# A decoder layer on one core: scores of two tiles on 32-row parts in mid-slot, expert weights asked for inside the experts' block

## Chip, cores and metric

One core of one Trainium2 chip runs the whole layer. The metric is the device time of one execution in microseconds (us). Engines are TensorE (PE), VectorE (DVE), ScalarE (ACT), GpSimd (POOL) and SyncE (SP, which here only issues DMAs).

## The reference

Input `x` is [64, 64, 256] (64 sequences of 64 tokens) and `ctx` is [64, 64, 64]. Three residual steps follow each other, all fp32:

```python
x = x + attn(layernorm(x))           # causal, 16 query heads, 4 key/value groups, head size 16
x = x + xattn(layernorm(x), ctx, ctx)  # no mask; keys and values are ctx; then @ Wc.T + bc
x = x + ffn(layernorm(x))            # 64 experts, top 6 of the best 3 of 8 groups, 96 slots each, and a shared MLP
# attn, xattn: softmax(q @ k.T / 4) @ v, for each head and each of the 64 sequences
# ffn: an expert computes (silu(x @ Wg.T) * (x @ Wu.T)) @ Wd.T on its slots; the shared MLP the same with 352 columns
```

## The kernel before

The 4096 tokens are 32 tiles of 128 tokens; a tile holds two sequences, and four tiles are a group. The program is a row of blocks; between two blocks all engines meet at a barrier: (1) inputs and constants, (2) attention (`attention_phase`), (3) a block in which SyncE issues the loads of the shared weights (`sgu`, `sd`) and of the first 8 experts' weights, (4) a block in which GpSimd writes seven small constants, (5) shared MLP and experts (`moe_phase`), (6) the final sums. An SBUF region that attention used is given to the weights only after block 2.

Block 2 does self attention for tiles 0 to 31 and cross attention for 32 to 63 in one software pipeline. Each engine runs `for m in range(FIRST, LAST)`, and the order of the calls in this loop body is the order of its queue; nothing but semaphores ties the engines. I call one turn `m` a slot. For each tile there are: scores (TensorE, line 396 the mask as a bf16 product, line 401 queries by keys, into `Sc`), their maximum and shift (VectorE, lines 724 and 728, into `E`), the exponential in place (ScalarE, 639), eight 128x128 transposes of it (TensorE, 413), copies to SBUF (ScalarE, 600), the product with the values (TensorE, 429, into the single bank `O`), reciprocal and output (VectorE, 735 and 744). Self attention adds the output to `X` on GpSimd (909); cross attention transposes it (439), multiplies it by `Wc` (447) and adds it to `X` on VectorE (753), and then routes the token: a third layer norm, logits (466), their transpose (474), choice of groups and experts on VectorE and GpSimd, and a transpose of the weights (482).

Queries lie in `qT` as two chunks of 128 rows, 8 heads of 16 rows each. Keys are copied by DMA from `kT` into `kbd`, where each head's 16 rows meet only the 64 columns of their own head, zeros elsewhere; this is 16 DMAs a group (line 275), all issued by SyncE, each with 16 partitions. TensorE's array is used in four parts of 64 by 64: `r` is the half of the rows, `b` the sequence. One product takes 64 rows (4 heads) and gives 256 columns. `Sc` has two buffers of two banks, used by tiles in turn. A product in fp32 goes through the array in two passes, so counts in the profile are twice those of the program.

Every other result of TensorE goes through a ring of 3 banks in the fixed order of `ring_uses` (unchanged); a bank is filled again when ScalarE or VectorE has saved the use three before.

Per slot TensorE does, in this order: scores of tile m+1, transpose of the output of m-2, transposes of tile m's exponentials, the `Wc` product of m-2, one or more of the group's projections and routing steps (by `m % 4`), and the value product of m-1. VectorE: maximum and shift of m+1, layer norm statistics, residual of m-2, reciprocal and output of m-1, routing steps. ScalarE: copies of tile m, layer norms and keys, exponential of m+1, queries.

## Time and profile before

| | us |
|---|---|
| median of 3 runs | 809.72 (807.61 to 810.27) |
| the profiled execution | 804.97 |
| its span | 803.2 |
| PE busy | 669.4 (83%) |
| PE weight loads busy | 483.4 (60%) |
| DVE busy | 479.0 (60%) |
| POOL busy | 351.2 (44%) |
| ACT busy | 337.6 (42%) |

Busy times are sums over the whole span. The probability transposes of tile 0 start at 41.51, those of tile 32 at 201.43; attention's last instruction on an engine ends at 434.96, and the experts' first matmul starts at 445.27. The granted clock is TensorE's, as a share of 2.4 GHz: 1.00 or 0.50 in any moment, 0.91 on average. "Idle before" in a row is how long the engine did nothing before it, with what ended the wait. A matmul's shown time contains its way through the array, so rows that follow closely overlap; what one costs is the distance from start to start.

### The profile page before, as it was taken

Reading aid. Unit: us, or ns where it says so; the run is one execution under the profiler, and the core shown is the slowest. Engines: PE = TensorE matmul, PEld = TensorE weight load, DVE = VectorE, ACT = ScalarE, POOL = GpSimd, SP = SyncE. Lnnn points to the kernel's source line nnn. Section 1 sums busy time; section 2 is a strip of 40 time slices with the busy share of each in tenths; the row PEclk is TensorE's granted clock in tenths of the full one; section 3 lists DMA queues with packets and bytes.
Section 4 is the critical chain, followed back from the end, with each engine's and each line's share of the span. In section 5 each row is a group of like instructions: output and inputs, shape, how many; then the busy total and the mean of one; then the engine's idle time right before and its main releaser. Section 6 shows DMA issues by size and latency. Waiting matters only on the chain. (4 is left out here: it accounts for less than half of the span.)

```text
span 803.2 us, 16833 instructions
## 1 busy us (share of the span) xinstructions
PE 669.4 (83%) x6353; PEld 483.4 (60%) x6353; DVE 479.0 (60%) x1087; ACT 337.6 (42%) x636; POOL 351.2 (44%) x356
## 2 busy tenths in 40 slices
PE   1699999997899897889761899979999999987093
PEld 0366666665676665657530355557788789976072
DVE  3267776677788687777753899742333334433058
ACT  2477777766687576565521232211222222221000
POOL 5021122225444234243120383383777777757354
PEclk9899999999999899998965799989999999999555
DMA  7234444554533232231113500013999999994299
GB/s 229 26 58 82 82 81 82 101 96 89 111 71 66 48 71 57 35 60 35 33 40 93 184 0 1 0 49 106 233 237 252 242 239 252 275 254 62 29 320 314
DMA packets 112063, 94.26 MB, mean 117 GB/s; under 512 B 59760, under 2 KB 95856, under 8 KB 111984
## 3 DMA queue, kind: packets, MB, share of 16 engines
q1 hardware_dynamic: 96368, 74.57, 36.7%
q0 software_dynamic: 10240, 14.16, 9.5%
q10 hardware_dynamic: 5376, 4.46, 1.8%
q8 instruction: 51, 0.84, 0.5%
q14 instruction: 28, 0.23, 0.1%
HBM read 60.26 MB, written 24.50 MB: 106 GB/s over the span
## 5 line engine op out<-in xcount | busy, mean ns | idle before, releaser
L1230 POOL DMA_INDIRECT sum_d<-nz,targets x64 | 91.8, 1434 | 40.5 <-DMA sum_d<-nz,targets 11.9
L724 DVE TENSOR_REDUCE mx<-Sc 128x16 f32<-128x1024 f32 x64 | 77.8, 1216 | 33.4 <-PE Sc L401 33.2
L1057 PE MATMUL bank<-xnT,sgu_sb 128*128 128x512 f32 (+1 forms) x192 | 87.7, 606 | 11.7 <-PEq L1593 11.7
L1112 PE MATMUL bank<-xT,wgu_sb 128*88 128x96 f32 x1024 | 95.8, 247 | 0.3 <-ACT xT L1181 0.3
L1112 PEld LDWEIGHTS bank<-xT,wgu_sb 128*88 128x88 f32 x1024 | 90.0, 158 | 0.6 <-issue 0.5
L600 ACT COPY ET<-ring 128x512 f32<-128x512 f32 x128 | 69.3, 589 | 42.5 <-PE ring L413 40.4
L1281 DVE TENSOR_TENSOR hid<-sil,bank 88x192 f32<-88x192 f32 x64 | 22.4, 350 | 104.2 <-ACT sil L1187 104.2
L413 PE MATMUL ring<-ident,E 128*128 128x128 f32 x512 | 72.6, 286 | 14.3 <-ACT E L639 13.4
L429 PEld LDWEIGHTS O<-vbd,ET 128*64 128x64 f32 x2048 | 69.2, 142 | 25.1 <-issue 17.2
L728 DVE TENSOR_TENSOR E<-Sc,mx 128x1024 f32<-128x1024 f32 x64 | 78.4, 1225 | 6.9 <-DVE mx L724 0.5
L639 ACT ACTIVATE E<-E 128x1024 f32<-128x1024 f32 x64 | 67.5, 1055 | 29.7 <-DVE E L728 29.5
L401 PE MATMUL Sc<-kbd,qT 64*64 64x256 f32 x1024 | 75.2, 399 | 4.5 <-DMA kbd<-kT 4.5
L413 PEld LDWEIGHTS ring<-ident,E 128*128 128x128 f32 x512 | 58.9, 146 | 30.8 <-ACT E L639 21.3
L429 PE MATMUL O<-vbd,ET 128*64 128x34 f32 x2048 | 76.4, 229 | 0.0
L1223 POOL DMA_INDIRECT xg<-rows_d,tokens x64 | 61.9, 967 | 27.9 <-issue 15.1
L1057 PEld LDWEIGHTS bank<-xnT,sgu_sb 128*128 128x128 f32 (+1 forms) x192 | 35.6, 186 | 54.0 <-issue 52.7
L909 POOL TENSOR_TENSOR X<-X,att 128x256 f32<-128x256 f32 x32 | 23.2, 726 | 101.7 <-DVE att L744 101.7
L1123 PE MATMUL bank<-wd_sb,hid 88*96 88x256 f32 x256 | 66.8, 384 | 0.0
L1063 PE MATMUL bank<-sd_sb,hT 128*128 128x256 f32 (+1 forms) x192 | 47.1, 398 | 6.6 <-POOL hT L1211 5.8
L735 DVE RECIPROCAL rc<-O 128x16 f32<-128x16 f32 x64 | 16.3, 255 | 56.9 <-PE O L429 56.7
L1181 ACT COPY xT<-bank 128x192 f32<-128x192 f32 x64 | 20.2, 318 | 71.1 <-PE bank L1100 71.1
L1405 PE MATMUL bank<-lastsb,wt 64*128 64x256 f32 x64 | 26.1, 636 | 26.6 <-DMA lastsb<-lasts_d 26.6
(152 smaller groups left out, 1139.0 us busy)
## 6 DMA issues: line engine op xcount, KB each, us to landing
wgu_sb<-in_wgu_dram SPq DMA_DIRECT2D x64, 352.0 KB
wd_sb<-in_wd_dram SPq DMA_DIRECT2D x64, 176.0 KB
sum_d<-zeros SPq DMA_DIRECT2D x16, 524.0 KB, 6.3
y<-sum_d SPq DMA_DIRECT2D x16, 512.0 KB, 8.8
kbd<-kT SPq DMA_DIRECT2D x248, 32.0 KB, 2.1
X<-in_x_dram SPq DMA_DIRECT2D x8, 512.0 KB, 6.5
rows_d<-xhT SPq DMA_DIRECT2D x8, 512.0 KB, 3.0
out_dram<-X ACTq DMA_DIRECT2D x8, 512.0 KB, 4.8
```

The source lines that it names most:

```text
L401: last = nc.tensor.matmul(Sc[m % 2][64 * b:64 * (b + 1), r, 256 * c:256 * (c + 1)], qT[rows, g % 2, c, at:at + 64], kbd[g % 2][rows, c, 2 ...
L413: last = nc.tensor.transpose(out[:, 128 * j:128 * (j + 1)], E_[:, m % 2, at:at + 128], ident[:])
L429: last = nc.tensor.matmul(O[64 * b:64 * (b + 1), 2 * VW * pair:2 * VW * (pair + 1)], ET[:, m % 2, j, 64 * b:64 * (b + 1)], vbd[:, g % 2, 2 ...
L600: nc.scalar.copy(ET[:, m % 2, 4 * v:4 * v + 4].rearrange("p j q -> p (j q)"), bank(name)[:]).then_inc(s_act, 1)
L639: nc.scalar.activation(E_[:, m % 2, :], E_[:, m % 2, :], ACT.Exp).then_inc(s_exp, 1)
L724: nc.vector.reduce_max(mx[:, m % 2, :], sc, AX.X).then_inc(s_mx, 1)
L728: nc.vector.tensor_tensor(E_[:, m % 2, :].rearrange("p (h k) -> p h k", k=S), sc, mx[:, m % 2, :].unsqueeze(2).to_broadcast([128, H, S]), ...
L1057: last = nc.tensor.matmul(out[0:m, :], sgu[:, e, k * MS + m0:k * MS + m0 + m], xnT[:, e, TOK * g:TOK * (g + 1)], start=e == 0, stop=e == 1)
L1112: last = nc.tensor.matmul(GP[e % 2][0:MH, CAP * u:CAP * (u + 1)], wgu[:, j, 4 * MH * c + MH * u:4 * MH * c + MH * (u + 1)], xT[:, e % 2, c ...
L1123: last = nc.tensor.matmul(DP[e % 2][0:CAP, 0:E], hid[:, e % 2, u, :], wd[:, j, E * u:E * (u + 1)], start=u == 0, stop=u == 1)
L1223: pool.indirect_dma_start(xg[:, j, :], None, w["rows"], bass.IndirectOffsetOnAxis(ap=tokens[:, e:e + 1], axis=0)).then_inc(s_g[j], 16)
L1230: pool.indirect_dma_start(w["sums"][e % 2], bass.IndirectOffsetOnAxis(ap=targets[:, e:e + 1], axis=0), outs[:, e % EB, :], None, compute_o ...
```

## The change

1. Scores are computed for two tiles in one call, `scores(p)` for tiles 2p and 2p+1. The array is used in eight parts: four strips of 32 rows (`r`, 2 heads each) by two halves of columns (`b`). One product takes 32 rows and gives 128 columns. Strip `r` writes bank `r` of `Sc`, which is now one buffer of four banks; tile n of the pair takes columns 256n to 256n+255 of each. The heads' order in `Sc` follows, and `pair_of` with it. The mask is 512 columns wide and is multiplied once for both tiles.
2. In TensorE's slot the value product of m-1 is now first; the scores stand behind the transposes of tile m, in even slots only, for tiles m+2 and m+3, and wait until both tiles before them are shifted.
3. Blocks 3 and 4 are gone. Their loads are the first DMAs, and their constants the first GpSimd instructions, of block 5; TensorE waits there for the three shared loads, VectorE for the constants where it uses them.

```diff
@@ -103,8 +103,8 @@
 def pair_of(j):
 
-    r, c, m = j // 4, j // 2 % 2, j % 2
-    return 4 * c + 2 * r + m
+    r, c = j // 2, j % 2
+    return 4 * c + r
 
@@ -381,27 +381,32 @@
                 last.then_inc(s_fill, 1)
 
-            def scores(m):
-                g, t = m // GT, m % GT
+            def scores(p):
+                g, t = 2 * p // GT, 2 * p % GT
                 cross = is_cross(g)
                 if t == 0:
                     pe.wait_ge(s_kbd, KDMA * (g + 1))
                     pe.wait_ge(*saved(("XT1" if cross else "Q1", g)))
-                if m >= 2:
-                    pe.wait_ge(s_sub, m - 1)
-                for c in range(2):
-                    if not cross:
-                        for r, b in ((0, 0), (1, 0), (0, 1), (1, 1)):
-                            rows = slice(64 * r, 64 * (r + 1))
-                            nc.tensor.matmul(Sc[m % 2][64 * b:64 * (b + 1), r, 256 * c:256 * (c + 1)],
-                                             ident_bf[rows, rows], mask[rows, :], start=True, stop=False)
-                    for r, b in ((0, 0), (1, 0), (0, 1), (1, 1)):
-                        rows = slice(64 * r, 64 * (r + 1))
-                        at = 128 * t + 64 * b
-                        last = nc.tensor.matmul(Sc[m % 2][64 * b:64 * (b + 1), r, 256 * c:256 * (c + 1)],
-                                                qT[rows, g % 2, c, at:at + 64],
-                                                kbd[g % 2][rows, c, 2 * t + b].rearrange("p h k -> p (h k)"),
-                                                start=cross, stop=True)
+                if p >= 1:
+                    pe.wait_ge(s_sub, 2 * p)
+                if not cross:
+                    for r in range(0, 4, 2):
+                        for k, b in ((0, 0), (1, 0), (0, 1), (1, 1)):
+                            rows = slice(64 * k, 64 * (k + 1))
+                            nc.tensor.matmul(Sc[64 * b:64 * (b + 1), r + k, :], ident_bf[rows, rows], mask[rows, :],
+                                             start=True, stop=False)
+                for n in range(2):
+                    for c in range(2):
+                        for b in range(2):
+                            at = 128 * (t + n) + 64 * b
+                            for r in range(4):
+                                rows = slice(32 * r, 32 * (r + 1))
+                                last = nc.tensor.matmul(
+                                    Sc[64 * b:64 * (b + 1), r, 256 * n + 128 * c:256 * n + 128 * (c + 1)],
+                                    qT[rows, g % 2, c, at:at + 64],
+                                    kbd[g % 2][rows, c, 2 * (t + n) + b, 2 * (r % 2):2 * (r % 2) + 2].rearrange(
+                                        "p h k -> p (h k)"), start=cross, stop=cross or (n == 1 and c == 1),
+                                    tile_position=(32 * r, 64 * b))
                 last.then_inc(s_sc, 1)
@@ -484,12 +489,14 @@
             pe.wait_ge(s_in, n_in)
             for m in range(FIRST, LAST):
-                if 0 <= m + 1 < 2 * NT:
-                    scores(m + 1)
+                if 0 <= m - 1 < 2 * NT:
+                    pv(m - 1)
                 if crossed(m - 2):
                     out_t(m - 2)
                 if 0 <= m < 2 * NT:
                     probs_t(m)
+                if m % 2 == 0 and 0 <= m + 2 < 2 * NT:
+                    scores(m // 2 + 1)
                 if crossed(m - 2):
@@ -520,8 +527,6 @@
                     if routed((m - 8) // 4):
                         logits((m - 8) // 4)
-                if 0 <= m - 1 < 2 * NT:
-                    pv(m - 1)
 
@@ -719,14 +724,15 @@
 
             def shift(m):
-                dve.wait_ge(s_sc, m + 1)
-                sc = Sc[m % 2][:].rearrange("p r (h k) -> p (r h) k", k=S)
-                nc.vector.reduce_max(mx[:, m % 2, :], sc, AX.X).then_inc(s_mx, 1)
+                dve.wait_ge(s_sc, m // 2 + 1)
+                sc = Sc[:, :, 256 * (m % 2):256 * (m % 2 + 1)].rearrange("p r (h k) -> p r h k", k=S)
+                nc.vector.reduce_max(mx[:, m % 2, :].rearrange("p (r h) -> p r h", r=4), sc, AX.X).then_inc(s_mx, 1)
                 if m >= 2:
                     dve.wait_ge(s_fill, ring.filled(("TP1", m - 2)))
                 dve.wait_ge(s_mx, m + 1)
-                nc.vector.tensor_tensor(E_[:, m % 2, :].rearrange("p (h k) -> p h k", k=S), sc,
-                                        mx[:, m % 2, :].unsqueeze(2).to_broadcast([128, H, S]),
+                nc.vector.tensor_tensor(E_[:, m % 2, :].rearrange("p (r h k) -> p r h k", r=4, k=S), sc,
+                                        mx[:, m % 2, :].rearrange("p (r h) -> p r h", r=4).unsqueeze(3).to_broadcast(
+                                            [128, 4, 4, S]),
                                         ALU.subtract).then_inc(s_sub, 1)
@@ -989,6 +995,9 @@
         return k if e % 2 == 0 and k < len(LATE) else None
 
+    s_in = sem("shared_weights")
+    s_one = sem("columns")
+    s_slot = sem("slots")
     s_up = sem("up")
@@ -1036,6 +1045,12 @@
                 sp.dma_start(w["lasts"][e:e + 1, :], outs[CAP - 1:CAP, e % EB, :]).then_inc(s_l[e % EB], 16)
 
+            sp.dma_start(sgu[:], w["sgu"].rearrange("(c p) n -> p c n", p=128)).then_inc(s_in, 16)
+            sp.dma_start(sd[:, 0:2, :], w["sd"][0:256].rearrange("(c p) n -> p c n", p=128)).then_inc(s_in, 16)
+            sp.dma_start(sd[0:MS - 256, 2, :], w["sd"][256:MS]).then_inc(s_in, 16)
+            for j in range(EB):
+                sp.dma_start(wgu[:, j, :], w["wgu"][j]).then_inc(s_w[j], 16)
+                sp.dma_start(wd[:, j, :], w["wd"][j]).then_inc(s_w[j], 16)
             for e in range(NE):
@@ -1124,7 +1139,7 @@
                 last.then_inc(s_d, 1)
 
-            pe.wait_ge(w["s_moe_in"], w["n_moe_in"])
+            pe.wait_ge(s_in, 48)
             early_up(0)
@@ -1231,6 +1246,15 @@
                                         outs[:, e % EB, :], None, compute_op=ALU.add).then_inc(s_s[e % 2], 16)
 
+            nc.gpsimd.iota(slot[:], pattern=[[1, CAP]], base=0, channel_multiplier=0,
+                           allow_small_or_imprecise_dtypes=True).then_inc(s_slot, 1)
+            nc.gpsimd.memset(own[:], 1.0).then_inc(s_one, 1)
+            nc.gpsimd.memset(lastone[:], 0.0).then_inc(s_one, 1)
+            nc.gpsimd.memset(lastrow[:], 0.0).then_inc(s_one, 1)
+            pool.wait_ge(s_one, 3)
+            for m, fill in ((own, 0.0), (lastone, 1.0), (lastrow, float(NT * 128 + CAP - 1))):
+                nc.gpsimd.affine_select(out=m[:], in_=m[:], compare_op=ALU.not_equal, fill=fill, base=-(CAP - 1),
+                                        pattern=[[0, 1]], channel_multiplier=1).then_inc(s_one, 1)
             hidden(0)
@@ -1325,6 +1349,7 @@
             nc.vector.tensor_scalar(mark[NE:128, :], top[NE:128, :], 0.0, None, ALU.is_equal).then_inc(s_tok, 1)
             dve.wait_ge(s_tok, 4)
+            dve.wait_ge(s_slot, 1)
             nc.vector.tensor_tensor(mark[NE:128, :], mark[NE:128, :], slot[NE:128, :], ALU.mult).then_inc(s_tok, 1)
@@ -1337,6 +1362,7 @@
             dve.wait_ge(s_tt, 1)
             nc.vector.tensor_copy(tokens[:], P[0][0:CAP, 0:NE]).then_inc(s_list, 1)
+            dve.wait_ge(s_one, 6)
             nc.vector.tensor_scalar(targets[:], P[0][0:CAP, 0:NE], own[:], lastrow[:], ALU.mult,
@@ -1472,7 +1498,7 @@
         mem["zeros"] = zeros = sb("zeros", [128, E + NE])
         mem["ident_bf"] = sb("ident_bf", [128, 128], BF16)
-        mem["mask"] = sb("mask", [128, HQ * S], BF16)
+        mem["mask"] = sb("mask", [128, HH * S], BF16)
         mem["halfmask"] = sb("halfmask", [128, 2])
@@ -1501,7 +1527,7 @@
         w["ctx2"] = sb("ctx2", [128, 2, GB, G * D])
 
-        mem["Sc"] = [pb(f"Sc{k}", [128, 2, 512]) for k in range(2)]
+        mem["Sc"] = pb("Sc", [128, 4, 512])
         mem["O"] = pb("O", [128, 512])
@@ -1528,7 +1553,7 @@
                     pool.wait_ge(s_const, h + 1)
                     nc.gpsimd.affine_select(out=m, in_=m, compare_op=ALU.is_ge, fill=MASKED,
-                                            base=0, pattern=[[0, HQ], [-1, S]],
+                                            base=0, pattern=[[0, HH], [-1, S]],
                                             channel_multiplier=1).then_inc(s_const, 1)
@@ -1568,19 +1593,6 @@
-        s_iota = ctx.enter_context(nc.semaphore("router_constants"))
-        w["s_moe_in"] = ctx.enter_context(nc.semaphore("shared_weights"))
-        w["n_moe_in"] = 48
-        with nc.Block() as block:
-            @block.sync
-            def _(sp):
-                sp.dma_start(w["sgu_sb"][:], sgu.rearrange("(c p) n -> p c n", p=128)).then_inc(w["s_moe_in"], 16)
-                sp.dma_start(w["sd_sb"][:, 0:2, :], sd[0:256].rearrange("(c p) n -> p c n", p=128)).then_inc(w["s_moe_in"], 16)
-                sp.dma_start(w["sd_sb"][0:MS - 256, 2, :], sd[256:MS]).then_inc(w["s_moe_in"], 16)
-                for j in range(EB):
-                    sp.dma_start(w["wgu_sb"][:, j, :], wgu[j]).then_inc(w["s_w"][j], 16)
-                    sp.dma_start(w["wd_sb"][:, j, :], wd[j]).then_inc(w["s_w"][j], 16)
...
@@ -1590,19 +1602,6 @@
-        with nc.Block() as block:
-            @block.gpsimd
-            def _(pool):
-                nc.gpsimd.iota(mem["slot"][:], pattern=[[1, CAP]], base=0, channel_multiplier=0,
...
```

On TensorE, the self half, from the keys projection of a group (`wkv_sb`) to the second query projection's neighbours; `ring<-ident,E` are the probability transposes, `O<-vbd,ET` the value products. Before:

```order
L356 MATMUL ring<-xhT,wkv_sb 128x512 x2
L429 MATMUL O<-vbd,ET 64x34 x16
L396 MATMUL Sc<-mask,ident_bf 64x256 x4
L401 MATMUL Sc<-kbd,qT 64x256 x4
L396 MATMUL Sc<-mask,ident_bf 64x256 x4
L401 MATMUL Sc<-kbd,qT 64x256 x4
L413 MATMUL ring<-ident,E 128x128 x8
L356 MATMUL ring<-xhT,wq_sb 128x512 x2
L429 MATMUL O<-vbd,ET 64x34 x16
```

and now:

```order
L356 MATMUL ring<-xhT,wkv_sb 128x512 x2
L434 MATMUL O<-vbd,ET 64x34 x16
L418 MATMUL ring<-ident,E 128x128 x8
L396 MATMUL Sc<-mask,ident_bf 64x512 x8
L404 MATMUL Sc<-kbd,qT 64x128 x32
L356 MATMUL ring<-xhT,wq_sb 128x512 x2
L434 MATMUL O<-vbd,ET 64x34 x16
L418 MATMUL ring<-ident,E 128x128 x8
```

The scores of one tile that stood between value products and transposes are gone from there; a pair's stand behind the transposes.

On TensorE, the cross half, one slot with `m % 4` = 0 of a routed group; `ring<-ident,att` is the transpose of the output, `wc_sb` the output projection, `gate` the logits. Before:

```order
L429 MATMUL O<-vbd,ET 64x34 x16
L401 MATMUL Sc<-kbd,qT 64x256 x8
L439 MATMUL ring<-ident,att 128x128 x2
L413 MATMUL ring<-ident,E 128x128 x8
L447 MATMUL ring<-wc_sb,oT 128x256 x2
L348 MATMUL ring<-ident,xh 128x128 x4
L466 MATMUL ring<-xnT,gate 64x512 x2
L429 MATMUL O<-vbd,ET 64x34 x16
```

and now:

```order
L434 MATMUL O<-vbd,ET 64x34 x16
L444 MATMUL ring<-ident,att 128x128 x2
L418 MATMUL ring<-ident,E 128x128 x8
L404 MATMUL Sc<-kbd,qT 64x128 x32
L452 MATMUL ring<-wc_sb,oT 128x256 x2
L348 MATMUL ring<-ident,xh 128x128 x4
L471 MATMUL ring<-xnT,gate 64x512 x2
L434 MATMUL O<-vbd,ET 64x34 x16
```

The scores moved from ahead of both transposes to between the transposes and the output projection, and the value products from the slot's end to its head.

## Rows read from the trace of the kernel before

**Rows 1.** TensorE in order of time, self half, one group: start us, us, what, [idle before]

```profile
117.54 1.10 PE L413 MATMUL ring<-ident,E 128*128 128x128 f32 x8
118.47 1.88 PE L356 MATMUL ring<-xhT,wkv_sb 128*128 128x512 f32 x4
120.28 1.13 PE L429 MATMUL O<-vbd,ET 128*64 128x34 f32 x32
121.34 0.30 PE L396 MATMUL Sc<-mask,ident_bf 64*64 64x256 bf16 x4
...
123.34 1.09 PE L413 MATMUL ring<-ident,E 128*128 128x128 f32 x8 [0.72 <-ACT E L639]
...
127.14 0.30 PE L396 MATMUL Sc<-mask,ident_bf 64*64 64x256 bf16 x4
...
128.34 1.09 PE L413 MATMUL ring<-ident,E 128*128 128x128 f32 x8
...
133.91 1.09 PE L413 MATMUL ring<-ident,E 128*128 128x128 f32 x8
...
138.27 1.10 PE L413 MATMUL ring<-ident,E 128*128 128x128 f32 x8
```

**Rows 2.** The key DMAs: SyncE's issues of one group; issues by size and us to landing

```profile
121.10 11.02 SPq L275 DMA_DIRECT2D kbd<-kT  x16
...
kbd<-kT SPq DMA_DIRECT2D x248, 32.0 KB, 2.1
```

**Rows 3.** TensorE where it waits for the key DMAs

```profile
195.95 1.09 PE L401 MATMUL Sc<-kbd,qT 64*64 64x256 f32 x16 [2.80 <-DMA kbd<-kT]
...
213.72 1.19 PE L401 MATMUL Sc<-kbd,qT 64*64 64x256 f32 x16 [1.68 <-DMA kbd<-kT]
...
215.31 1.91 PE L413 MATMUL ring<-ident,E 128*128 128x128 f32 x8
```

**Rows 4.** Engines per stretch: us, busy (instructions) PE, PEld, DVE, ACT, POOL, clock, DMA

```profile
197.91:218.37 20.46, 17.53 (x248) 13.82 (x247) 16.60 (x30) 14.13 (x26) 10.79 (x11) 0.92 0.58 115
218.37:237.40 19.03, 18.11 (x260) 14.28 (x259) 16.78 (x36) 14.74 (x28) 7.38 (x11) 1.00 0.40 78
260.14:288.97 28.83, 24.86 (x279) 18.63 (x278) 21.70 (x70) 17.66 (x35) 10.57 (x14) 0.88 0.28 55
```

**Rows 5.** TensorE in order of time, cross half, no routing

```profile
219.74 1.09 PE L401 MATMUL Sc<-kbd,qT 64*64 64x256 f32 x16
220.79 0.41 PE L439 MATMUL ring<-ident,att 128*128 128x128 f32 x2
...
221.91 1.03 PE L447 MATMUL ring<-wc_sb,oT 128*128 128x256 f32 x4
```

**Rows 6.** VectorE in order of time, cross half, no routing

```profile
224.85 0.42 DVE L744 TENSOR_TENSOR att<-O,rc 128x256 f32<-128x256 f32 x1
...
227.03 1.22 DVE L728 TENSOR_TENSOR E<-Sc,mx 128x1024 f32<-128x1024 f32 x1
...
233.13 0.41 DVE L753 TENSOR_TENSOR X<-ring,X 128x256 f32<-128x256 f32 x1
...
233.81 0.42 DVE L744 TENSOR_TENSOR att<-O,rc 128x256 f32<-128x256 f32 x1
```

**Rows 7.** All engines in order of time, cross half, fully routed group

```profile
275.89 0.41 DVE L753 TENSOR_TENSOR X<-ring,X 128x256 f32<-128x256 f32 x1
...
276.35 1.11 PE L482 MATMUL ring<-ident,wa 128*128 128x128 f32 x4 [2.46 <-DVE X L753]
```

**Rows 8.** All engines between attention and experts; the shared weights' landing

```profile
436.19 0.46 SPq L1579 DMA_DIRECT2D sd_sb<-in_sd_dram  x1
...
444.08 0.22 POOL L1596 IOTA slot<- 128x96 f32 x1 [11.77 <-DVEq L1593]
...
445.27 1.19 PE L1057 MATMUL bank<-xnT,sgu_sb 128*128 128x512 f32 x1 [11.72 <-PEq L1593]
...
sd_sb<-in_sd_dram SPq DMA_DIRECT2D x1, 96.0 KB, 4.6
```

18 lines of the change are left out of this document (4 added, 14 removed).

## Prediction

> **What bounds the kernel now.** I read the time in four stretches, and the change touches two of them: attention (0 to 435 us) and the gap between attention and the experts (435 to 445 us). I call turn `m` of the attention loop a slot; A, B, C, D are the slots with `m % 4` = 0, 1, 2, 3, and four slots serve one group of four tiles.
>
> In the self half TensorE is the bound. In [rows 1] the probability transposes, once per slot, start 5.80, 5.00, 5.57 and 4.36 us apart, 20.73 for a group, and the only idle time is 0.72 us in front of slot A's. It waits there for ScalarE, which must first copy this group's keys and values out of the bank: keys projection at 118.47, transposes at 123.34, held by the exponential of line 639. Keys then go through 16 DMAs that SyncE issues one after the other in 11.02 us, each landing 2.1 us after its issue [rows 2]: at 118.47 plus 15.1 to 15.8.
>
> In the cross half the bound moves. Two groups wait for those DMAs; after one such wait of 1.68 us the granted clock was at its lower level, 1.2 GHz, and eight transposes took 1.91 us for 1.09 [rows 3]. A group without routing takes 19.03 us, one with all of it 28.83 us at a mean granted clock of 0.88 [rows 4]. In the latter VectorE is 21.70 us busy, against 16.78, and TensorE sits 2.46 us waiting for VectorE's residual addition to free a bank [rows 7]. So the cross half is a loop between TensorE and VectorE, and its order matters more than TensorE's work.
>
> **Scores of two tiles at once.** A tile's scores cost 1.20 us in the self half (127.14 to 128.34) [rows 1], 1.05 us in the cross half (219.74 to 220.79) [rows 5]. Each of 4 array parts then streams 4 times 256 fp32 columns. Now each of 8 parts streams 8 times 128 columns for a pair of tiles: as many columns a part, twice the tiles. So a pair should cost what one tile did, 1.05 us; in the self half the mask passes keep their columns (0.15 a tile, so 0.30) and one more change of part size is passed, for which I take 0.1: 1.45 us. That saves 1.05 and 0.95 us a pair. The bound above: the value products issue 32 passes in 1.06 us (120.28 to 121.34) [rows 1], 33 ns each, and a pair now has 64: 2.1 us, no saving. I take the lower end, since those passes have 34 columns and load new weights each, and share the array by 2 where this has 8 parts.
> The Trainium skill, "TensorE: Matmul & The Clock Gate", section "Wait — 56ns, not 53.3ns?", has a rule against such small pieces: where the sequencer decodes in microcode, each matmul takes it 62 ns, whatever its columns; by that, 64 would cost 4.0 us a pair and the whole come to some 60 us more. The 33 ns of the value products disagree with it here, so it changes no term, and its chance is under 0.01, inside rival (c).
>
> **The new order, self half.** A slot's own work is unchanged but for the scores: A 5.00 - 1.20 + 1.45 = 5.25, B 5.57 - 1.20 = 4.37, C 4.36 - 1.20 + 1.45 = 4.61, D 5.80 - 0.72 - 1.20 = 3.88: 18.1 us for 20.73. But two things do not get shorter. (1) Slot A's transposes wait for ScalarE until 123.34 - 118.47 = 4.87 us after the keys projection began. Before, value products and one tile's scores (2.26) filled this; now only value products stand there (the scores moved behind the transposes), so TensorE idles 4.87 - 1.81 - 1.06 = 2.0 us where it idled 0.72. Period: 20.1. (2) The first scores of a group now come in slot C, not at the start of D. From the keys projection to there it is 4.87 + 0.93 + 1.45 + 1.81 + 4.37 + 1.99 = 15.4 us, and the DMAs land after 15.1 to 15.8: a wait of 0 to 0.4. So a group takes 20.1 to 20.5, and six of them save 2.4 us of the 15 that the work alone would give. The start costs the 1.45 us of the first pair, which now stands as a whole ahead of the value transposes and the second keys: +1.4. And an idle stretch of 2.0 us can cost the clock: it fell after 1.68 in [rows 3], and not after every such wait. That one lasted some 3.3 us (a mean clock of 0.92 over the 20.46 us around it [rows 4]) and cost up to half of that: 1.7. I count two among the six groups, +3.4. Self half together: +2.4.
>
> **Cross half.** Here VectorE's maximum and shift of slot m's next tile must be done before the pair's scores in A and C (one buffer instead of two), the output projection `wc` stands behind these scores, VectorE's residual behind `wc`, then reciprocal and output, and TensorE's value products, now first in the slot, behind the output. It is one chain through both engines. From output to output in A or C: end of output to end of shift 2.98 (225.27 to 228.25) [rows 6], to the scores 0.1, scores 1.05, `wc` 1.03 [rows 5], residual to end of output 1.10 (233.13 to 234.23) [rows 6] and 0.05 between: 6.3. In B or D: 0.1, value products 1.06, transposes 1.12 (220.79 to 221.91), `wc` 1.03, 1.15: 4.5. Two of each are 21.6 us for a group without routing, where [rows 4] has 19.03: +2.6. The groups before it wait for DMAs anyway, and value products now lie between the scores and the next keys: +1.1 and, with the residual's chain, +1.8; the partly routed one +0.5. A fully routed group adds VectorE's 21.70 - 16.78 = 4.9 us in the same chain: 26.5; 1.0 for falls of the clock, which the old ones have too: 27.5 for 28.83, 28.0 and 28.3 (the two routed groups that follow it), so -2.7 for three. In the last two groups and the drain no next scores hold the chain, and the last value products come ahead of `wc` (1.03) and of a logits projection (4 passes of 0.43) instead of behind them: 3 us, and 2 for scores and shifts that no longer alternate; -5, between -2 and -7. Cross half: +1.1 + 1.8 + 2.6 + 0.5 - 2.7 - 5 = -1.7.
>
> **Between attention and experts.** The last attention instruction but a DMA ends at 435; the last piece of the shared weights is asked for at 436.19, but TensorE starts at 445.27, since SyncE first issues 16 more weights, then the block ends, then GpSimd writes its constants in another [rows 8]. Now TensorE waits for the shared weights alone: issue at 436.19 and 4.6 us to landing: 440.8. Gain 4.4. VectorE starts its 12 rounds of maxima 10 us earlier, but they ended ahead of TensorE before, so this gives nothing more. GpSimd's seven small constants lie beside that wait. All behind it is bound by TensorE's own queue and shifts as a whole. The longer mask costs GpSimd up to 1 us at the very start, while VectorE clears the key buffer until 5.4: nothing; without that cover, 1 us.
>
> **Sum.** +2.4 - 1.7 - 4.4 = -3.7 on the profiled 804.97 (span 803.2 and 1.8 around it), which lies 4.75 below the median of the three runs, 809.72. On the median: **806.0**. A difference of 0.3%, 2.4 us, is about what a measurement of this kernel can tell from none.
>
> **Rivals.**
> (a) *The clock falls in every self group.* The 2.0 us idle ahead of slot A is new in each. Eight falls of 1.7 us instead of two: +10.2, so 816. For it: the row after 1.68 us of waiting. Against: the wait of 2.80 us ahead of 195.95 left the clock alone [rows 3]. It decides against the change from about four falls on.
> (b) *The cross loop is looser than I chain it.* If VectorE runs a slot ahead and the scores find their buffer free, groups with routing are bound by VectorE's work or TensorE's, some 22 to 24 us, and those without stay at 19: 27.5 becomes 23 for each of three, -13.5, and the 2.6 of the group without routing may stay as well: 790 to 793. For it: VectorE waits for value products in all groups now, and no more then. Against: the shift stands behind the output in VectorE's own queue [rows 6].
> (c) *The eight parts do not run side by side*, so the change does not do what it says: a pair costs 2.1 and all 32 pairs lie on a chain: +1.0 each, 838. Against: four parts do so now, eight transfers of weights are small.
> (d) *The gap does not close*: the weights land later, as 17 transfers share the queues: +4.4, 810. Against: these same transfers were in flight before.
>
> **Chances.** Forecast 0.48 (its own range 798 to 811: DMA wait 0 to 0.4 a group, falls of the clock 0 to 4, drain -2 to -7), (a) 0.18, (b) 0.20, (c) 0.07, (d) 0.04, the rest 0.03. Faster by over 0.3% (below 807.3): 0.29 of the forecast's, all of (b), a little of (a): 0.51. Within: 0.21. Slower: 0.28. Range: 791 to 817, which leaves out (c) and the far ends.
>
> **What would show it.** Right: a pair of scores in about 1.05 us (cross) and 1.45 (self); 2.0 us idle ahead of every slot A's transposes in the self half, with ScalarE's exponential named; group periods of 20.1 to 20.5, then 21.6, then 26 to 28; TensorE waiting for VectorE's shift ahead of the scores and for its output ahead of the value products; the experts' first matmul 5.6 us after attention ends. Wrong: self groups of 18 us (ScalarE's chain shorter than read) or over 21 (clock); routed groups near 22 or over 29; a pair's scores at 2 us.

## The result, and the profile after

| | before | changed |
|---|---|---|
| median of 4 runs, us | 808.71 (807.61 to 810.27) | 817.89 (815.08 to 818.63) |
| ratio to before | | 1.0106, 95% interval 1.0074 to 1.0138 |
| profiled execution, us (span) | 804.97 (803.2) | 818.63 (816.9) |

The changed kernel is 1.1% slower. It was forecast at 806.0 us in a range of 791 to 817. The two profiled spans differ by 13.7 us, more than the medians (9.2): the profiled execution of before was faster than all four of the table, and that of the changed kernel was the slowest of its four. The page of the changed kernel:

```profile
span 816.9 us, 18604 instructions
...
PE 652.5 (80%) x7249; PEld 482.8 (59%) x7249; DVE 475.0 (58%) x1087; ACT 339.0 (41%) x636; POOL 352.1 (43%) x356
...
L434 PE MATMUL O<-vbd,ET 128*64 128x34 f32 x2048 | 75.2, 227 | 21.4 <-DVE att L750 18.6
...
L418 PE MATMUL ring<-ident,E 128*128 128x128 f32 x512 | 71.2, 284 | 16.8 <-ACT E L644 16.4
...
L404 PE MATMUL Sc<-kbd,qT 32*64 32x128 f32 x2048 | 44.0, 308 | 24.0 <-DVE E L733 16.7
```

And two lines of the page before:

```profile
L401 PE MATMUL Sc<-kbd,qT 64*64 64x256 f32 x1024 | 75.2, 399 | 4.5 <-DMA kbd<-kT 4.5
...
L429 PE MATMUL O<-vbd,ET 128*64 128x34 f32 x2048 | 76.4, 229 | 0.0
```

TensorE's own work fell from 669.4 to 652.5 us, the scores alone from 75.2 us (1024 passes) to 44.0 (2048 passes), and the kernel still got slower: the time went into waits, named at the end of the rows. TensorE was idle for 4.5 us ahead of scores and not at all ahead of value products; now it is 24.0 and 21.4 us, most of it spent on VectorE. The same group of the self half as in [rows 1], TensorE in order of time (start us, us, what, [idle before]):

```profile
131.44 1.10 PE L418 MATMUL ring<-ident,E 128*128 128x128 f32 x8 [1.93 <-ACT E L644]
132.47 0.63 PE L396 MATMUL Sc<-mask,ident_bf 64*64 64x512 bf16 x8
133.02 1.21 PE L404 MATMUL Sc<-kbd,qT 32*64 32x128 f32 x64
134.16 1.98 PE L356 MATMUL ring<-xhT,wq_sb 128*128 128x512 f32 x4
...
152.56 0.66 PE L418 MATMUL ring<-ident,E 128*128 128x128 f32 x4 [1.93 <-ACT E L644]
```

A pair's scores take 0.55 us for the mask and 1.14 for 64 passes (132.47, 133.02, 134.16). With two such pairs, and with 1.93 us of idle time ahead of slot A for 0.72, a group takes 21.12 us for 20.73. TensorE where the cross half waits, against [rows 3] and [rows 5]:

```profile
207.03 2.01 PE L404 MATMUL Sc<-kbd,qT 32*64 32x128 f32 x64 [4.05 <-DMA kbd<-kT]
208.97 1.93 PE L434 MATMUL O<-vbd,ET 128*64 128x34 f32 x32
210.83 1.97 PE L418 MATMUL ring<-ident,E 128*128 128x128 f32 x8
...
227.86 1.21 PE L404 MATMUL Sc<-kbd,qT 32*64 32x128 f32 x64 [1.94 <-DMA kbd<-kT]
...
238.87 1.21 PE L404 MATMUL Sc<-kbd,qT 32*64 32x128 f32 x64 [0.53 <-DVE E L733]
...
242.44 1.13 PE L434 MATMUL O<-vbd,ET 128*64 128x34 f32 x32 [0.87 <-DVE att L750]
...
250.70 1.21 PE L404 MATMUL Sc<-kbd,qT 32*64 32x128 f32 x64 [1.36 <-DMA kbd<-kT]
```

The first cross group's keys now cost a wait of 4.05 us for 2.80, and the value products behind it take 1.93 us for 1.13. The second group's keys cost 1.94 us for 1.68. In the group without routing TensorE waits for VectorE's shift (0.53), for its output (0.87) and once more for keys (1.36). Three stretches follow, as in [rows 4]: 10 us from the last microsecond of the first wait on, the group without routing, and the first fully routed one:

```profile
206.00:216.00 10.00, 8.13 (x138) 7.19 (x138) 6.58 (x12) 3.74 (x7) 4.28 (x4) 0.50 0.75 148
237.30:260.70 23.40, 17.95 (x333) 15.14 (x331) 17.41 (x38) 15.95 (x30) 8.89 (x11) 1.00 0.34 67
284.66:313.21 28.55, 22.15 (x345) 17.71 (x344) 21.75 (x71) 17.98 (x33) 10.83 (x14) 0.94 0.29 57
```

The clock was at 1.2 GHz (0.50) in all of the first; no such stretch followed the 2.80 us of [rows 3]. The group without routing takes 23.40 us (19.98 before, from the transposes of slot 36 to those of slot 40), the routed one 28.55 (29.10 before, 264.82 to 293.92). The end of attention and the start of the experts, for [rows 8]:

```profile
450.43 0.69 DVE L827 SCALAR_TENSOR_TENSOR keys<-desc,ring 64x512 f32<-64x512 f32 x1 [2.80 <-ACT wt L640]
451.41 0.39 SPq L1048 DMA_DIRECT2D sgu_sb<-in_sgu_dram  x1
...
452.36 0.46 SPq L1050 DMA_DIRECT2D sd_sb<-in_sd_dram  x1
...
457.90 2.08 PE L1072 MATMUL bank<-xnT,sgu_sb 128*128 128x512 f32 x2 [8.18 <-DMA sd_sb<-in_sd_dram]
```

All engines are through the barrier 0.3 us after attention's last instruction (451.13), and TensorE starts 6.8 us behind it, for 10.3: the blocks' merging gave 3.5 us. The account by stretches; a stretch is given by the slots whose transposes begin and end it:

| stretch | changed minus before, us | forecast |
|---|---|---|
| start to slot 0 | +2.3 | +1.4 |
| slots 0 to 24 (six self groups) | +6.6 | +1.0 |
| 24 to 32 | +5.75 | +1.1 |
| 32 to 36 | +1.6 | +1.8 |
| 36 to 40 (no routing) | +3.4 | +2.6 |
| 40 to 44 | +0.2 | +0.5 |
| 44 to 56 (three routed groups) | -2.5 | -2.7 |
| 56 to attention's end | -1.2 | -5 |
| gap | -3.5 | -4.4 |
| experts to the end | +1.0 | 0 |

### The profile page after: what moved, and what is told of

Same layout as the page of the kernel before. It is cut to its first block and busy times, and to the rows that moved or that the text cites. A ratio compares the mean times of both kernels' runs of the same rounds, so it can differ in the third digit from the quotient of the medians.

```text
span 816.9 us, 18604 instructions
## 1 busy us (share of the span) xinstructions
PE 652.5 (80%) x7249; PEld 482.8 (59%) x7249; DVE 475.0 (58%) x1087; ACT 339.0 (41%) x636; POOL 352.1 (43%) x356
## 5 line engine op out<-in xcount | busy, mean ns | idle before, releaser
L434 PE MATMUL O<-vbd,ET 128*64 128x34 f32 x2048 | 75.2, 227 | 21.4 <-DVE att L750 18.6
L418 PEld LDWEIGHTS ring<-ident,E 128*128 128x128 f32 x512 | 58.3, 144 | 20.2 <-ACT E L644 18.1
L404 PE MATMUL Sc<-kbd,qT 32*64 32x128 f32 x2048 | 44.0, 308 | 24.0 <-DVE E L733 16.7
L404 PEld LDWEIGHTS Sc<-kbd,qT 32*64 32x64 f32 x2048 | 35.5, 148 | 35.0 <-issue 16.0
L1202 ACT ACTIVATE sil<-bank 88x192 f32<-88x192 f32 x64 | 20.9, 326 | 77.5 <-PE bank L1127 66.3
L1078 PEld LDWEIGHTS bank<-sd_sb,hT 128*128 128x128 f32 (+1 forms) x192 | 38.1, 200 | 15.3 <-issue 9.6
```

The source lines that it names most:

```text
L404: last = nc.tensor.matmul(Sc[64 * b:64 * (b + 1), r, 256 * n + 128 * c:256 * n + 128 * (c + 1)], qT[rows, g % 2, c, at:at + 64], kbd[g % 2 ...
L418: last = nc.tensor.transpose(out[:, 128 * j:128 * (j + 1)], E_[:, m % 2, at:at + 128], ident[:])
L434: last = nc.tensor.matmul(O[64 * b:64 * (b + 1), 2 * VW * pair:2 * VW * (pair + 1)], ET[:, m % 2, j, 64 * b:64 * (b + 1)], vbd[:, g % 2, 2 ...
L1078: last = nc.tensor.matmul(out, hT[0:m, c, 128 * t:128 * (t + 1)], sd[0:m, c, :], start=c == 0, stop=c == 2)
```

## The experiments

Each was timed against the kernel before on the same chip; ratios are to that kernel. One ratio is uncertain by 0.3 to 0.4%, and so a difference between two of them by some 3 to 4 us. The changed kernel stands at 1.0106.

### Merged blocks alone

Edit: parts 1 and 2 of the change left out, part 3 kept.

> The kernel before with the merged blocks alone. Theory: the gap between attention and the experts closes as it did in the changed kernel, 10.3 us before, 6.8 us there, and nothing else moves: 3.5 us faster than before. Rival: the earlier start is partly given back behind it, because in the changed kernel the stage from the experts' first matmul to the end took 359.0 us for 357.9: 2.4 us faster, and second rival, all of it is given back: no difference.

Measured: ratio 0.9961, interval 0.9928 to 0.9993, some 3 us less; attention's end to the experts' first matmul 437.02 to 443.13, 6.1 us. The blocks' merging is a gain near the 3.5 us expected; the first rival's 2.4 cannot be told from it. The new scores alone therefore cost 1.0106 / 0.9961, 11.7 us, uncertain by some 4. That is what has to be explained.

### The new order with the old parts

```diff
+            def scores(p):
                 if p >= 1:
                     pe.wait_ge(s_sub, 2 * p)
...
                 for n in range(2):
-                    for c in range(2):
...
+                    tile_scores(2 * p + n)
```

`tile_scores` is the old function for one tile, with 64-row parts and two banks, without its wait for the shift; the layout of `Sc`, `pair_of` and the mask are the old ones.

> The changed kernel (merged blocks, pairs of scores in mid-slot, value product first) with the old parts of 64 rows and the old layout of the scores. Theory 'order': the place of the scores costs the time and the parts of 32 rows are a gain of their own, 0.96 us a pair in the cross half (2.10 for 1.14) and 0.5 in the self half (2.4 for 1.9): 16 x 0.96 + 16 x 0.5 = 23 us slower than the changed kernel, some 841. Theory 'parts': the small parts cost what the trace does not show and the order is harmless: no slower than the changed kernel, 818 or less.

Measured: 1.0398 (1.0355 to 1.0440), 23.5 us slower than the changed kernel. TensorE in the self half (a pair in C, then slot A) and the cross half (a pair):

```profile
155.01 0.30 PE L394 MATMUL Sc<-mask,ident_bf 64*64 64x256 bf16 x4
...
157.30 0.66 PE L348 MATMUL ring<-ident,xh 128*128 128x128 f32 x4
...
165.66 1.97 PE L417 MATMUL ring<-ident,E 128*128 128x128 f32 x8 [1.93 <-ACT E L643]
167.56 0.43 PE L394 MATMUL Sc<-mask,ident_bf 64*64 64x256 bf16 x4
...
255.58 1.96 PE L399 MATMUL Sc<-kbd,qT 64*64 64x256 f32 x32 [0.53 <-DVE E L732]
257.46 1.13 PE L451 MATMUL ring<-wc_sb,oT 128*128 128x256 f32 x4
```

A pair on 64-row parts takes 2.29 us in the self half (155.01 to 157.30, 1.69 on 32-row parts) and 1.88 in the cross half (1.14). The small parts are a gain of 0.6 us a pair in the self half and 0.75 in the cross half. For the cross half I had expected 0.96. If all pairs lay on the path, 16 x 0.75 + 16 x 0.6 = 22 us would be the whole, but part of the 23.5 is the clock: the transposes behind 1.93 us of idle time take 1.90 us (165.66 to 167.56) in slots 0, 4, ... 24, in all seven, where the changed kernel has three such slots. Four more falls of 1.5 us are 6 us. So the expected sum was hit by another mix, which is luck. What holds is that the small parts are a gain and the order is the loss: with the same 64-row parts, the new order is 35 us slower than the merged blocks alone.

### Pairs on small parts at the head of the odd slots

```diff
-                if 0 <= m - 1 < 2 * NT:
-                    pv(m - 1)
+                if m % 2 == 1 and 0 <= m + 1 < 2 * NT:
+                    scores((m + 1) // 2)
                 if crossed(m - 2):
                     out_t(m - 2)
                 if 0 <= m < 2 * NT:
                     probs_t(m)
-                if m % 2 == 0 and 0 <= m + 2 < 2 * NT:
-                    scores(m // 2 + 1)
...
+                if 0 <= m - 1 < 2 * NT:
+                    pv(m - 1)
```

> The changed kernel with pairs of scores on 32-row parts at the head of the odd slots (tiles m+1 and m+2) and the value product back at the slot's end. Theory 'order': TensorE no longer waits in mid-slot for VectorE's shift, the first scores of a group stand again where they stood, a slot later, so that the key DMAs have landed in the self half and cost 2.8 and 1.7 us again instead of 4.05, 1.94 and 1.36: at least 12 us faster than the changed kernel, 800 to 806. Theory 'parts': the order is harmless, the same as the changed kernel within 3 us, 815 to 821. The idle time of about 2 us ahead of slot A's transposes is expected to stay by both, since no scores stand at the head of slot A.

Measured: 1.0134 (1.0094 to 1.0174), 2 us above the changed kernel and not separable from it. The expectation "order" fell. The first wait for keys was gone, but the second had become 3.48 us. A self group took 20.86 us for the old 20.73: what the group saved on the scores stood as idle time ahead of slot A (1.93 for 0.72). And the routed groups became longer than in either kernel (29.1 before, 28.55 changed). The first of them, and its waits:

```profile
271.11:302.68 31.57, 24.93 (x344) 20.32 (x343) 22.18 (x72) 17.95 (x33) 10.81 (x14) 0.79 0.28 55
```

```profile
282.63 1.11 PE L487 MATMUL ring<-ident,wa 128*128 128x128 f32 x4 [2.34 <-DVE X L759]
...
286.58 0.66 PE L444 MATMUL ring<-ident,att 128*128 128x128 f32 x2 [0.98 <-DVE att L750]
```

With less work of its own, TensorE only comes earlier to VectorE's residual addition (`X`) and output (`att`), idles 2.34 and 0.98 us there, and the clock of the group is 0.79. What the small parts save is worth nothing where VectorE or ScalarE sets the period. That the idle time also brings the lower clock is a reading of this trace; no run took it out here.

### Half of the cross half's key DMAs

```diff
-for c in range(1 if g == 0 else 2):
+for c in range(1 if g == 0 or g >= NG else 2):
```

The waits' counts follow. It leaves out the keys of heads 8 to 15 in cross attention. The second of the two runs has the same edit on the kernel with merged blocks and the old scores.

> The changed kernel, in which the cross half's keys are copied for the first 8 heads alone (8 DMAs a group instead of 16; the other heads' scores use what lies in the buffer). Theory 'key DMAs': the waits of 4.05, 1.94 and 1.36 us ahead of a group's first scores vanish, and the lower clock behind the first of them (a mean of 0.65 over the 15 us around it) with them: 8 to 10 us faster than the changed kernel. Rival 'chain': VectorE's shift, one buffer for two tiles, takes the place of each wait: 2 us faster at most.

> The kernel before with merged blocks, in which the cross half's keys are copied for the first 8 heads alone (8 DMAs a group; the other heads' scores use what lies in the buffer). In the changed kernel this was worth 10 us by the medians. Theory: the old order waits less for the key DMAs, 2.81 and 1.74 us in two groups and one fall of the clock of 1.7: at most 6 us faster than the same kernel with all keys, so that at least 4 of the changed kernel's loss are the earlier place of a group's first scores. Rival: it gains as much here, 10 us, and the place of the scores has nothing to do with it.

Measured: in the changed kernel 0.9981 (0.9954 to 1.0008), 10.1 us less; with the old scores and merged blocks 0.9865 (0.9830 to 0.9900) for 0.9961, 7.8 us less. Slots 24 to 44 took 110.97 us in the changed kernel and 99.39 with half its key DMAs, 100.15 with the old scores and 94.51 with half. So the key DMAs bound both orders: 11.6 us of these slots go in the new, 5.6 in the old. Of the 11.6, 1.5 is the fall of the clock in slot 24, ahead of any wait for these keys, and in the new order one wait of 0.89 us for keys remains. Of the 10.8 us between the two kernels 4.9 stay with half of the DMAs, which I put down to the new order's chain. The second result lies between its two cases, at most 6 us and 10, and by its uncertainty decides for neither.

### The idle time ahead of slot A filled

```diff
-                pe.wait_ge(s_exp, m + 1)
                 for v in range(2):
                     out = empty_bank((f"TP{v}", m))
+                    if v == 0:
+                        if m % 4 == 0 and m <= NT:
+                            for j in range(14):
+                                nc.tensor.transpose(out[:, 128 * (j % 4):128 * (j % 4 + 1)], ident[:], ident[:])
+                        pe.wait_ge(s_exp, m + 1)
```

> The changed kernel with 14 transposes of the identity, into the ring bank that the next real transposes overwrite, where TensorE idles 1.93 us ahead of slot A's transposes (tiles 0, 4, ... 32): some 1.6 us of filling that delays nothing. Theory 'clock': the lower clock in slot A (7.18 us instead of 5.69 in three of the seven groups of the changed kernel, in all seven of the one with parts of 64 rows) comes from this idle time: every slot A of the self half takes 5.69 us, 3 to 4.5 us faster than the changed kernel. Rival: the falls have another cause: they stay, and the time is the same or up to 1 us longer.

Measured: 1.0059 (1.0031 to 1.0086), 3.8 us less than the changed kernel, uncertain by 3.4. TensorE at slot 12, and slots 0 to 24 (busy times, clock, DMA), first with the filling:

```profile
106.14 1.75 PE L418 MATMUL ring<-ident 128*128 128x128 f32 x14
108.15 1.09 PE L422 MATMUL ring<-ident,E 128*128 128x128 f32 x8 [0.26 <-ACT E L648]
...
113.83 1.09 PE L422 MATMUL ring<-ident,E 128*128 128x128 f32 x8
```

```profile
44.03:171.58 127.55, 125.12 (x2077) 88.12 (x2077) 82.82 (x138) 92.27 (x144) 25.83 (x44) 1.00 0.40 77
```

And in the changed kernel:

```profile
43.80:173.69 129.89, 118.13 (x1992) 80.76 (x1993) 83.10 (x138) 92.25 (x144) 25.79 (x44) 0.97 0.42 75
```

With 1.75 us of useless transposes in the gap, slot A takes 5.7 us in all seven groups (108.15 to 113.83) and the mean clock is 1.00 for 0.97. In the changed kernel three slots A (0, 12, 24) took 7.18 us, 1.5 more, and three other kernels with the same self half have three such slots each. So the clock falls do come from this idle time: there is more work on the same path, and it takes less time.

### The value product first, scores tile by tile

```diff
             for m in range(FIRST, LAST):
+                if 0 <= m - 1 < 2 * NT:
+                    pv(m - 1)
                 if 0 <= m + 1 < 2 * NT:
                     scores(m + 1)
...
-                if 0 <= m - 1 < 2 * NT:
-                    pv(m - 1)
```

On the kernel with merged blocks.

> The kernel before with merged blocks and one move: the value product first in the slot, ahead of the next tile's scores, which stay per tile on 64-row parts. Theory 'value product': the shorter routed groups of the changed kernel (28.5, 27.0, 26.7 us against 29.1, 27.8, 27.9 before) and its shorter end come from this move: the same lengths here, 3 us faster than the merged blocks alone; the self half keeps its 20.7 us a group. Rival 'pairs': they come from scores computed once in two slots: groups of 28 to 29 us here, no faster than the merged blocks alone or slower.

Measured: 1.0492 (1.0455 to 1.0529), 43 us slower than the merged blocks alone. The rival allowed for slower, but with routed groups of 28 to 29 us; these took 26.05, 25.14 and 26.05 us, less than in any kernel so far. Both follow from one chain. TensorE and VectorE over one self slot:

```profile
149.22 1.13 PE L429 MATMUL O<-vbd,ET 128*64 128x34 f32 x32 [1.32 <-DVE att L744]
150.28 0.30 PE L396 MATMUL Sc<-mask,ident_bf 64*64 64x256 bf16 x4
...
151.48 1.09 PE L413 MATMUL ring<-ident,E 128*128 128x128 f32 x8
...
155.55 0.27 PE L429 MATMUL O<-vbd,ET 128*64 128x34 f32 x3 [0.69 <-DVE att L744]
```

```profile
148.65 0.42 DVE L744 TENSOR_TENSOR att<-O,rc 128x256 f32<-128x256 f32 x1
151.63 1.22 DVE L724 TENSOR_REDUCE mx<-Sc 128x16 f32<-128x1024 f32 x1 [2.56 <-PE Sc L401]
152.96 1.22 DVE L728 TENSOR_TENSOR E<-Sc,mx 128x1024 f32<-128x1024 f32 x1
...
154.65 0.23 DVE L735 RECIPROCAL rc<-O 128x16 f32<-128x16 f32 x1
154.98 0.42 DVE L744 TENSOR_TENSOR att<-O,rc 128x256 f32<-128x256 f32 x1
```

The scores end at 151.5. VectorE's maximum and shift follow, 1.22 us each; behind them in its queue stand statistics (not shown), the reciprocal and the output, which ends at 155.4. Only then comes TensorE's next value product (it waits 0.69 for `att`), and behind that the next scores. The chain goes round once in every slot, 6.33 us, where a self slot has 4.4 to 5.6 of work. The changed kernel has the same chain, but with scores in only one of two slots; that this is what the pairs are good for is argued and not tested. A routed slot of the merged blocks alone takes 7 us on average. There the chain costs nothing, and TensorE's waits for `X` in three routed groups shrink from 10.2 us in total to 1.8.

### The new order only from slot 42 or 44 on

Two versions on the kernel with merged blocks. The first switches to the changed kernel's pairs for tiles 44 and up, the second only calls `pv(m - 1)` first from slot 44 on:

```diff
             for m in range(FIRST, LAST):
+                if 44 <= m and m - 1 < 2 * NT:
+                    pv(m - 1)
...
-                if 0 <= m - 1 < 2 * NT:
+                if 0 <= m - 1 < 43:
                     pv(m - 1)
```

> The old scores (64-row parts, tile by tile at the head of the slot, value product at its end) for tiles 0 to 43, pairs on 32-row parts in mid-slot with the value product first from tile 44 on, and the merged blocks. Theory: the new order and parts are worth what the two traces show for the routed groups and the end (slot 44 to the last keys 166.5 us in the changed kernel, 170.1 before), and the loss lies all ahead of them: 3.7 for this and 3.5 for the blocks, 7 us faster than before. Rival: the gain there hangs on the state in which the loop enters, or is lost in the scatter of the clock: no faster than the merged blocks alone, 3.5 us faster than before.

> The kernel before with merged blocks, and the value product first in the slot from slot 44 on (before that at the slot's end). Theory: where the value product stands first for the whole loop, TensorE and VectorE form one chain a slot (maximum, shift, output, value product, scores: 6.3 us), which costs much in the self half and nothing where a slot takes 6.3 us anyway; there it shortened a routed group from 29.2, 27.8 and 27.8 us to 26.1, 25.1 and 26.1, and slot 60 to the last keys from 58 to 60 us to 52.5. So from slot 44 on 7.5 + 2.3 + 6 = 16 us less, 1 to 2 of them lost at the change of order: 14 us faster than the merged blocks alone, 18 faster than before. Rival: the short groups hang on the long ones ahead of them, that is on work already done when the loop arrives: at most 4 us faster than the merged blocks alone.

Measured: 0.9953 (0.9926 to 0.9979) for the pairs, no more than the merged blocks alone (0.9961), so the rival held. In its trace slot 42, where the order changes, took 10.47 us for 5.96. And 0.9793 (0.9758 to 0.9828) for the value product first, 13.6 us less than the merged blocks alone, as expected: routed groups of 26.69, 26.36 and 26.06 us, and 51.6 us from slot 60 to attention's end (60.4 with the merged blocks alone).

### The keys earlier

```diff
                     if is_self((m + 6) // 4):
                         xt((m + 6) // 4, 1)
+                    if is_cross((m + 6) // 4):
+                        keys((m + 6) // 4)
...
                 elif m % 4 == 3:
-                    if 0 <= (m + 5) // 4 < 2 * NG:
+                    if is_self((m + 5) // 4):
                         keys((m + 5) // 4)
```

The cross groups' key transposes move from slot D to slot C, on ScalarE and in the ring's order as well. In two of the four kernels SyncE's order changes, too:

```diff
+                block_keys(g)
                 if NG - 1 <= g < 2 * NG - 1:
                     load_ctx(g - NG + 1)
-                block_keys(g)
```

> The changed kernel with the transposes of the cross half's keys one slot earlier, nothing else. Theory 'the new place of the scores asks for the keys a slot too early': the waits of 4.05, 1.94 and 1.36 us vanish as in the run with half the DMAs: 8 to 10 us faster than the changed kernel, with the right result. Rival: what the half of the DMAs saved was not the waits but the traffic, or ScalarE's turn: 3 us faster at most.

> The one before, and the transposes of the cross half's keys one slot earlier (slot C instead of D), so that SyncE starts on a group's key DMAs some 4 us earlier. Theory 'key DMAs': the waits of 2.8 and 1.7 us and the fall of the clock behind one of them vanish: 5 to 8 us faster than the one before; half the DMAs gave 7.7. Rival: the chain through SyncE does not start earlier, because the copy in ScalarE's queue or the free key buffer comes last: within 1 us of the one before.

> The changed kernel with the cross half's key transposes one slot earlier, and SyncE's loads of a later group's context behind a group's key DMAs instead of ahead of them. Theory: what was left of the waits (3.55 us for the second cross group) stood in SyncE's queue behind the context, which waits for its buffer: all waits for keys vanish, 7 to 10 us faster than the changed kernel, as with half the DMAs. Rival: SyncE's 16 issues of 0.7 us each are as long as a light group lets them be, in whatever order: within 3 us of the changed kernel.

> The kernel before with merged blocks, value product first from slot 44 on, the cross half's key transposes one slot earlier and the context's loads behind the keys'. Theory: its wait of 4.55 us for the second cross group's keys and the fall of the clock behind it vanish, 5 us less than without the last change: 0.969 of the time before. Rival: no difference from the run without it, 0.975.

| kernel | ratio (interval) | compared with |
|---|---|---|
| changed, keys earlier | 1.0091 (1.0058 to 1.0124) | 1.0106 |
| changed, keys earlier, context behind | 1.0036 (1.0002 to 1.0070) | 1.0106 |
| value product first from 44, keys earlier | 0.9753 (0.9728 to 0.9778) | 0.9793 |
| the same, context behind | 0.9761 (0.9718 to 0.9804) | 0.9753 |

In the changed kernel the first edit gave 1.2 us, not the 8 to 10 expected: it moved a wait instead of removing it. The 4.05 us were gone (scores at 204.26 without a wait for keys), but the second group's 1.94 had become 3.55, at the lower clock (2.02 us a pair). SyncE's own rows tell a part of why. TensorE, then SyncE of that kernel:

```profile
225.46 2.02 PE L406 MATMUL Sc<-kbd,qT 32*64 32x128 f32 x64 [3.55 <-DMA kbd<-kT]
```

```profile
201.70 1.28 SPq L282 DMA_DIRECT2D sum_d<-zeros  x2
209.88 0.37 SPq L296 DMA_DIRECT2D ctxA<-in_ctx_rows_dram  x1
...
212.27 11.67 SPq L277 DMA_DIRECT2D kbd<-kT  x16
```

SyncE was through with everything at 202.98 and stood for 6.9 us at the context of a later group, whose buffer was still read; the keys behind it were issued from 212.27 on, right behind the context's three DMAs. With the context behind the keys:

```profile
201.81 0.60 SPq L296 DMA_DIRECT2D ctxA<-in_ctx_rows_dram  x1
...
209.38 10.96 SPq L277 DMA_DIRECT2D kbd<-kT  x16
```

they go out from 209.38 on, so the context had cost 2.9 of the 6.9 us; they still wait for something else until then. No wait for keys is left in the whole cross half, and the changed kernel is 5.6 us faster than it was, uncertain by some 4. All 16 DMAs are still there, so the gain is that of the waits and not of less traffic. It is below the 7 to 10 expected, which the uncertainty doesn't exclude; TensorE now waits 1.46 us for the context in slot 26 instead, with the lower clock behind it. In the kernel with the value product first, the keys earlier gave 3.2 us of the 5 to 8 expected, which can't be told from nothing: its waits of 3.20, 0.75 and 2.49 us became one of 4.55 in slot 34. SyncE's new order exchanged that one for two of 1.76 and 1.57 us for the context, and gave nothing.

The kernel with merged blocks, value product first from slot 44 and keys a slot earlier is the fastest found by its ratio, 786.40 us for 806.50 on the same chip, 2.5% faster than before and 3.5% faster than the changed kernel. A routed group in it, and below it one of the merged blocks alone:

```profile
267.10:292.25 25.15, 21.69 (x281) 16.62 (x279) 21.95 (x71) 17.64 (x33) 10.84 (x15) 1.00 0.32 64
```

```profile
294.60:322.36 27.76, 23.48 (x280) 17.39 (x279) 21.86 (x71) 17.77 (x33) 10.81 (x14) 0.94 0.30 58
```

VectorE's 22 us are the same. The group is 2.6 us shorter, and the clock is at its higher level in all of it.

## Why the prediction failed, point by point

The forecast had a gain of 3.7 us and the profiled time rose by 13.7.

**Right.** The eight parts run side by side: 1.14 us a pair for the 1.05 taken, rival (c) is out. On the rule of the Trainium skill against small pieces the runs are as clear as the value products were: 64 passes in 1.14 us are 18 ns each, not 62. The same section of the Trainium skill ("TensorE: Matmul & The Clock Gate", "Wait — 56ns, not 53.3ns?") also says that matmuls never start closer than some 25 ns apart; an estimate by that is 1.6 us a pair, and the trace disagrees with this as well. The idle time ahead of slot A (2.0, measured 1.93, by ScalarE's exponential), slot B (4.37, measured 4.36), the size and the number of clock falls there (1.7 and two, measured 1.5 and two up to slot 24), TensorE's waits for VectorE's shift and output in the cross half, and the three routed groups (-2.7, measured -2.5) came as worked out. The gap gave less (-4.4, measured -3.5): from the last shared weight's issue to TensorE's start it took 5.5 us, not 4.6. The start cost 2.3 us for 1.4; 0.45 of it is the pair's term below, and kernels with the same start reach slot 0 between 43.3 and 45.5 us.

**1.45 us a pair in the self half.** This term was mis-sized. The mask takes 0.55 us, not 0.30: I had it as the difference of two whole scores, 0.15 a tile, where the mask's own steps in that trace were 0.13 and 0.11 us, 0.24 a tile (from 127.14 and from 127.70). The passes take 1.14, and the steps on both sides grew by 0.2 (the transposes ahead 1.03 for 0.93, the projection behind 1.92 for 1.81), together 1.9. Slot D came out 0.25 longer, too. So there are 19.19 us of work, not 18.1, and 0.39 more a group instead of 0.4 less: 4.7 us over six groups. No wait of a group's first scores for its keys came on top. The prediction's sign "over 21 (clock)" was met by the groups of 21.12 us, but not for its reason: the clock didn't fall in them. The six groups also carry 1.06 us that is no loss: slot 0 now holds a value product that stood behind it.

**"The groups before it wait for DMAs anyway": +1.1 for slots 24 to 32.** This is the step that failed most: +5.75. That the keys land as late as before while the first scores ask for them a slot earlier was right, but I priced only the longer wait (1.25 us more) and put what it does to the clock at nothing. Behind 4.05 us of waiting all of the next 10 us ran at 1.2 GHz. Against the run with half of the DMAs, slots 30 to 33 took 7.5 us more, of which the wait is 4.05; the rest, 3 to 4 us, is what I take for the clock, and a part of it lies in the stretch behind. Slot 24 had a fall of 1.5. I had charged clock falls to the self half and 1.0 to a routed group. The runs with half the DMAs and with SyncE's new order put 5.6 to 10 us of the changed kernel's time on late keys.

**"In the last two groups and the drain no next scores hold the chain": -5.** They do: the pairs for tiles 60 to 63 are computed in slots 58 and 60, and wait there for VectorE's shift. TensorE of the changed kernel:

```profile
383.41 2.01 PE L404 MATMUL Sc<-kbd,qT 32*64 32x128 f32 x64 [1.96 <-DVE E L733]
...
397.45 1.21 PE L404 MATMUL Sc<-kbd,qT 32*64 32x128 f32 x64 [1.46 <-DVE E L733]
```

Slots 56 to 60 took 27.97 us for 27.02, slots 60 and 61 together 13.29 for 12.73. Only the drain was shorter, 42.9 us from slot 62 for 45.6. Measured: -1.2.

**+2.6 for the group without routing.** The chain was right, 6.47 and 4.54 us for A and B (6.3 and 4.5 forecast), but a third group waited for its keys, 1.36 us, where I let only the first two wait. The group took 23.40 us for the 21.6 forecast. That the difference (+3.4) is not further off comes from a second error: the 19.03 us that I took for it in the old kernel were another stretch, and slots 36 to 40 took 19.98.

The 11.7 us of the new scores are then 3.8 for the clock in the self half (by the filling), 2.3 for its longer steady groups (six times 0.39, from the trace) and 5.6 for late keys (by the key transposes a slot earlier and SyncE's order); the rest of the table cancels. The first and the last are uncertain by 3 to 4 us each, so that the sum fits so well is partly luck. Rival (a) had named 816 us, near the measured 817.9, but not for what happened: it wanted a fall of the clock in every self group, and up to slot 24 there were two.

**Open.** No run has the filling and SyncE's new order together, so that the two gains add up is not shown. Why the clock falls in seven of seven slots A with 64-row parts and in three with 32-row parts, at the same idle time, was not tried. Nor was the small part tile by tile in the old order: four strips take four banks in this layout, and two buffers of that size would be eight beside those of the ring and `O`. The stage of the experts took between 355.7 and 360.8 us in kernels in which it is the same code, so its +1.0 is not explained by the change.

## What to carry to other kernels

Work taken from an engine is a gain only where that engine ends the period: here the cheaper scores became idle time in which TensorE waits for VectorE and ScalarE. Idle time that lengthens can take the clock with it, at a price above what it lengthened by: 1.25 us more of waiting for keys cost 3 to 4 us at the lower clock. Before moving a step earlier, list every queue that must have delivered for it, and read in that queue's own rows what stands ahead of the delivery. And an order need not be one for the whole loop: the same move of one call cost 43 us over the whole and gave 14 in its last third.

## What the runs showed of the hardware

- On eight parts of 32 by 64, fp32 passes of 128 columns start 18 ns apart on average (64 in 1.14 us); on four parts of 64 by 64 those of 256 columns start 66 ns apart (16 in 1.05, one tile) or 59 (32 in 1.88, two tiles without a break).
- 1.75 us of useless transposes in an idle stretch of 1.93 made the kernel 3.8 us faster: from slot 0 to slot 24 the clock stayed at 2.4 GHz (a mean of 1.00 for 0.97).
- SyncE's queue takes 0.69 us to issue each of these 32 KB key DMAs, 11 us a group, while slots 28 to 32 and 32 to 36 take 15.8 and 16.2 us in the old order with half of them. A context load that waited 6.9 us in that queue for a free buffer made the keys behind it 2.9 us later (212.27 for 209.38).
